# A decoder block on one core: where the mixture's last combining stands against the first group tile's work, and when two projection matrices are loaded

## What is computed

```python
# mixture (third sublayer); input is the normed x
logits = nf @ gate_weight.T + gate_bias
scores, idx = top_k(logits, 2);  w = softmax(scores)
g, lin = min(p1[..., 0::2], 7), clip(p1[..., 1::2], -7, 7)   # p1 = nf @ mlp1 + bias
act = g * sigmoid(1.702 * g) * (lin + 1)
p2 = act @ mlp2 + bias
combined = sum over the two experts of w * p2
x = x + (xc + combined)
# grouped attention (fourth sublayer), twice: groups of 32 neighbours, then of 32 strided rows
q, k, v = x @ wqs, x @ wks, x @ wvs                          # 16 heads of 64
out = softmax(q k^T / 8) v - v
x = layernorm(out @ pw + pb + x);  x = layernorm(relu(x @ w1 + b1) @ w2 + b2 + x)
```

## Time and profile before

| what | value |
|---|---|
| median of 3 runs | 2058.28 us (2058.02 to 2059.34) |
| profiled execution | 2049.87 us, span 2048.1 us |
| PE busy | 1867.4 us, 91% |
| DVE busy | 1302.1 us, 64% |
| ACT busy | 973.7 us, 48% |
| POOL busy | 966.9 us, 47% |
| DMA, mean | 59 GB/s |

### The profile page before, as it was taken

How to read it: one execution, slowest core, us unless ns; L and a number is a source line. 1 busy time by engine, 2 the same in 40 slices (tenths; PEclk the granted TensorE clock), 3 DMA queues, 4 the chain that set the end, 5 groups by cost and what they waited for, 6 DMA issues and landing times.

```text
span 2048.1 us, 52534 instructions
## 1 busy us (share of the span) xinstructions
PE 1867.4 (91%) x21476; PEld 1548.2 (76%) x21476; DVE 1302.1 (64%) x2932; ACT 973.7 (48%) x1984; POOL 966.9 (47%) x783
## 2 busy tenths in 40 slices
PE   7999999999999999977649389999999999988994
PEld 5677777777777777756437379999899999987883
DVE  6667676767676766637756565456556554556883
ACT  3666666666666666532236144334443343335551
POOL 2555555555555555535644633344234333435440
PEclk9999999999999999999869689999999999999996
DMA  7101020101230100135234520000220000220000
GB/s 245 52 17 50 19 78 19 50 19 70 101 129 19 50 11 12 40 127 167 73 101 126 153 90 13 16 20 13 80 79 28 19 18 18 71 88 17 12 17 16
DMA packets 74606, 119.85 MB, mean 59 GB/s; under 512 B 8392, under 2 KB 64464, under 8 KB 70992
## 3 DMA queue, kind: packets, MB, share of 16 engines
q1 hardware_dynamic: 69392, 105.31, 15.3%
q0 software_dynamic: 2560, 6.30, 1.1%
q10 hardware_dynamic: 2416, 4.88, 0.6%
HBM read 76.61 MB, written 39.85 MB: 57 GB/s over the span
## 4 chain that ended last, share of the span: by engine, by line
PE 41%; DVE 4%; POOL 4%; issue 3%; DMA 2%; ACT 2%; SPq 0%; POOLq 0%; DVEq 0%
PE psum L265 12%; PE psum L276 9%; PE psum L2000 4%; PE psum L1988 2%; PE psum L2492 2%; PE psum L1974 2%; PE psum L225 1%; PE psum L2526 1%; POOL b_yg L1472 1%; PE psum L1248 1%; PE psum L1338 1%; PE psum L1355 1%; POOL xs L1462 1%; PE psum L246 1%; ACT e_pr L2631 1%
## 5 line engine op out<-in xcount | busy, mean ns | idle before, releaser
L770 POOL TENSOR_TENSOR a_sm<-a_sm,a_rsum 128x1024 f32<-128x1024 f32 x256 | 480.2, 1895 | 357.1 <-DVE a_rsum L804 354.7
L792 DVE CUSTOM_DVE_ANT_0 a_sm<-psum,a_strip 128x1024 f32<-128x1024 f32 x256 | 312.1, 1219 | 145.6 <-PE psum L624 145.5
L705 ACT ACTIVATE a_sm<-a_sm,a_mn 128x1024 f32<-128x1024 f32 x256 | 293.9, 1148 | 27.3 <-DVE a_mn L792 26.2
L710 ACT ACTIVATE a_pT<-psum 128x512 f32<-128x512 f32 x256 | 151.6, 592 | 274.7 <-PE psum L637 274.7
L637 PE MATMUL psum<-ident,a_sm 128*128 128x128 f32 x2048 | 275.9, 277 | 5.7 <-POOL a_sm L770 4.6
L637 PEld LDWEIGHTS psum<-ident,a_sm 128*128 128x128 f32 x2048 | 224.4, 141 | 63.2 <-issue 46.3
L652 PE MATMUL psum<-a_pT,a_V 128*64 128x256 f32 x2048 | 249.0, 385 | 0.6 <-ACT a_o L716 0.6
L652 PEld LDWEIGHTS psum<-a_pT,a_V 128*64 128x64 f32 x2048 | 136.1, 136 | 77.3 <-issue 22.1
L799 DVE COPY a_pT<-psum 128x512 f32<-128x512 f32 x256 | 175.0, 684 | 13.3 <-PE psum L637 6.1
L2084 ACT ACTIVATE g_val<-psum 128x512 f32<-128x512 f32 x64 | 38.0, 598 | 225.5 <-PE psum L2000 225.5
L624 PE MATMUL psum<-a_KH,a_QH 64*128 64x512 f32 x512 | 114.5, 444 | 2.5 <-DVE a_mn L792 2.5
(11 more groups left out here) (394 smaller groups left out, 3733.8 us busy)
## 6 DMA issues: line engine op xcount, KB each, us to landing
a_strip<-table SPq DMA_DIRECT2D x16, 960.0 KB, 6.6
oT<-a_o SPq DMA_DIRECT2D x64, 128.0 KB, 1.9
xs<-b_zeros SPq DMA_DIRECT2D x8, 1024.0 KB, 4.1
b_oT_in<-oT SPq DMA_DIRECT2D x8, 1024.0 KB, 5.6
y<-b_yb SPq DMA_DIRECT2D x23, 256.0 KB, 2.2
b_xs<-xs SPq DMA_DIRECT2D x23, 128.0 KB, 2.2
a_raw<-in_a_wqkv SPq DMA_DIRECT2D x7, 384.0 KB, 3.3
s_x<-in_x_rev SPq DMA_DIRECT2D x4, 512.0 KB, 8.0
```

The source lines that it names most:

```text
L705: a.activation(sm[:, st % RING, :], sm[:, st % RING, :], ACT.Exp, scale=-1.0, bias=mn[:, at:at + 1], accum_out=rsum[:, at:at + 1]).then_in ...
L710: a.activation(probs(st, 0), psum[:, 4, :].rearrange("p (k q) -> p k q", k=4), ACT.Copy).then_inc(sig("pT_act"), 1)
L770: g.tensor_tensor(sm[:, st % RING, :], sm[:, st % RING, :], rsum[:, at:at + 1].broadcast_to([P, T]), ALU.mult).then_inc(sig("scaled"), 1)
L792: v.tensor_tensor_reduce(out=sm[:, st % RING, :], in0=scores_banks(hl).rearrange("p c n -> p (c n)"), in1=strip[:, pair % 2, hl, qt * P:qt ...
```

## The change

SP issues the two projection matrices in turn 5 of its unit loop (ahead of fetch_sorted(8)) and no longer ahead of the loop. At the end of the mixture, DVE does the norm sums and the scaling of tile 0 between combined(0) and combined(1), the low columns of tile 0 behind combined(1), sums, norm of tile 1 and all four key evictions of tile 0 ahead of combined(4). combined(5), (6) and (7) go into the grouped attention's step s = 0: behind the first half's `inverse`, behind the second half's `inverse`, and behind the second `transposed`. On POOL the root of tile 1 and the residual of tile 0 stand between gather(3) and gather(4), and gather(7) stands between the probabilities of the first and of the second half.

```diff
--- before.py
+++ after.py
@@ -1229,8 +1229,9 @@
         sp.wait_ge(routed("sc"), 16 * 2 * PT * NP)
         for j in range(UR):
             fetch_sorted(j)
-        then["load_projections"](sp)
         for j in range(NU + 2):
+            if j == 5:
+                then["load_projections"](sp)
             if j + UR < NU:
                 fetch_sorted(j + UR)
             if j >= 2:
@@ -1515,10 +1516,15 @@
         for r in range(UR):
             g.wait_ge(sig(f"sy{r}"), 16 * len(range(r, NU, UR)))
         g.wait_ge(sig("tables"), 2 + KC)
-        for s in range(NP):
+        for s in range(4):
             gather(s)
             if s == 1:
-                then["first_root"](g)
+                then["root"](g, 0)
+        then["root"](g, 1)
+        then["residual"](g, 0)
+        for s in range(4, 7):
+            gather(s)
+        return gather
 
     def vector(v, then):
         chain = Chain(v, sig("v_chain"))
@@ -1734,18 +1740,18 @@
         then["low_part"](v, 1)
         then["low_part"](v, 2)
         combined(0)
-        then["first_stats"](v)
+        then["first_stats"](v, 0)
+        then["first_norm"](v, 0)
         combined(1)
-        then["first_norm"](v)
+        then["low_columns"](v)
+        then["first_stats"](v, 1)
         combined(2)
-        then["low_columns"](v)
         combined(3)
+        then["first_norm"](v, 1)
+        then["first_keys"](v, (0, 1))
+        then["first_keys"](v, (2, 3))
         combined(4)
-        combined(5)
-        then["first_keys"](v, (0, 1))
-        combined(6)
-        then["first_keys"](v, (2, 3))
-        combined(7)
+        return combined
 
     return {"signals": [sig, have], "routed": routed, "where": where, "following": following, "turns": turns, "sync": sync, "tensor": tensor,
             "scalar": scalar, "gpsimd": gpsimd, "vector": vector}
@@ -2131,21 +2137,21 @@
                     high_part(a, 0, W1)
                     high_part(a, 0, W2)
 
-    def first_root(g):
-        norm_rstd(g, sig, "dl", 0, dl, mhalf)
-
-    def gpsimd(g, then):
-        def residual(s):
-            r = s % 2
-            if local(s):
-                g.wait_ge(sig("dl_h"), PT * (s + 1))
-            else:
-                loaded(g, s)
-            if s >= 2:
-                g.wait_ge(sig("dy_out"), s - 1)
-            g.wait_ge(have("vec"), 32)
-            g.tensor_tensor(eb[:, r, :, :], e[:, r, :, :], over_tiles(vec[:, phase(s), 0, :], PT), ALU.add).then_inc(sig("e_pb"), 1)
-
+    def root(g, s):
+        norm_rstd(g, sig, "dl", s, dl, mhalf)
+
+    def residual(g, s):
+        r = s % 2
+        if local(s):
+            g.wait_ge(sig("dl_h"), PT * (s + 1))
+        else:
+            loaded(g, s)
+        if s >= 2:
+            g.wait_ge(sig("dy_out"), s - 1)
+        g.wait_ge(have("vec"), 32)
+        g.tensor_tensor(eb[:, r, :, :], e[:, r, :, :], over_tiles(vec[:, phase(s), 0, :], PT), ALU.add).then_inc(sig("e_pb"), 1)
+
+    def gpsimd(g, then, gather):
         chain = Chain(g, sig("g_chain"))
 
         def result(s):
@@ -2160,7 +2166,6 @@
                 last = g.tensor_tensor(w[:, :, :], w[:, :, :], x[:, r, :, :], ALU.add)
             last.then_inc(sig("result"), 1)
 
-        residual(0)
         for s in range(NG + 1):
             front, back = s < NG, s > 0
             if back:
@@ -2172,10 +2177,12 @@
                 if s > 1:
                     g.wait_ge(sig("fy_out"), s - 1)
                 g.tensor_tensor(zb[:, :, :], z[:, :, :], over_tiles(vec[:, phase(s - 1), 3, :], PT), ALU.add).then_inc(sig("a1_b2"), 1)
-            if s + 1 < NP:
-                norm_rstd(g, sig, "dl", s + 1, dl, mhalf)
+            if 0 < s < NP - 1:
+                root(g, s + 1)
             if front:
                 for t in range(PT):
+                    if t and not s:
+                        gather(NP - 1)
                     n = PT * s + t
                     g.wait_ge(sig("d_inv"), n + 1)
                     g.tensor_tensor(pr[:, t, :, :], pr[:, t, :, :], spread(mx[:, t, :], SEG),
@@ -2184,7 +2191,7 @@
                     g.tensor_tensor(pr[:, t, :, :], pr[:, t, :, :], over_tiles(eye[:, :], H0),
                                     ALU.subtract).then_inc(sig("d_probs"), 1)
             if s + 1 < NG:
-                residual(s + 1)
+                residual(g, s + 1)
             if s == NG - 1:
                 then["first_roots"](g)
             if 0 < s < NG:
@@ -2223,7 +2230,7 @@
         v.tensor_tensor(both[:, 1, :, :], halves(banks(stage, n)), both[:, 0, :, :].bitcast(F32),
                         ALU.subtract).then_inc(sig(f"{stage}_out"), 1)
 
-    def vector(v, then):
+    def vector(v, then, combined):
         chain = Chain(v, sig("v_chain"))
 
         def shifted(s, t):
@@ -2304,12 +2311,14 @@
                 low_part(v, 1, WQ)
             if s == NP + 1:
                 low_part(v, 1, W2)
-            if s + 1 < NP:
+            if 0 < s < NP - 1:
                 first_sums(v, s + 1)
                 first_norm(v, s + 1)
             if front:
                 shifted(s, 0)
                 inverse(s, 0)
+            if not back:
+                combined(NP - 3)
             if back:
                 low_columns(v, "fT", s - 1, zT)
             if not front:
@@ -2320,6 +2329,8 @@
                 low_columns(v, "dT", s + 1, eT)
             if front:
                 inverse(s, 1)
+                if not back:
+                    combined(NP - 2)
                 transposed(s, 0)
             if back:
                 low_hidden(s - 1, (0,))
@@ -2328,6 +2339,7 @@
             if back:
                 low_hidden(s - 1, (1,))
             if not back:
+                combined(NP - 1)
                 low_part(v, 0, PW)
             if back:
                 low_hidden(s - 1, (2, 3))
...
@@ -2953,13 +2965,13 @@
 
             @block.gpsimd
             def _(g):
-                mixture["gpsimd"](g, groups)
-                groups["gpsimd"](g, last)
+                gather = mixture["gpsimd"](g, groups)
+                groups["gpsimd"](g, last, gather)
 
             @block.vector
             def _(v):
-                mixture["vector"](v, groups)
-                groups["vector"](v, last)
+                combined = mixture["vector"](v, groups)
+                groups["vector"](v, last, combined)
     return groups["signals"] + last["signals"] + [mixture["routed"]]
```

More of the change, by code:

```diff
@@ L2353, in group_attentions @@
             "high_part": lambda a, i: high_part(a, 0, i), "first_columns": lambda a: high_columns(a, 0),
-            "first_queries": lambda a, units: scaled_queries(a, 0, units), "first_root": first_root,
-            "first_stats": lambda v: first_sums(v, 0), "first_norm": lambda v: first_norm(v, 0),
+            "first_queries": lambda a, units: scaled_queries(a, 0, units), "root": root,
+            "residual": residual, "first_stats": first_sums, "first_norm": first_norm,
             "low_part": lambda v, i: low_part(v, 0, i), "low_columns": lambda v: low_columns(v, "dT", 0, eT),
```

## The result

The changed kernel took 2060.48 us (median of 22 runs, 2056.32 to 2069.71), the kernel before, run between them, 2055.3 us (22 runs, 2047.0 to 2062.66). The ratio is 1.0033, with a 95% interval of 1.0022 to 1.0045: slower by 6.8 us, between 4.5 and 9.2 (the two medians by themselves differ by 5.2, the two means by 6.4). The forecast was +0.5 us.

A forecast was written before the change was run, and what follows sets the result against it. PE, 91% busy, was taken as the bound, so only its stalls in units and seam could give time. Terms 0 - 1.7 + 1.7 + 0.5 = +0.5 us gave 2058.8 from the median 2058.28; range 2054 to 2062.5.

The forecast's parts named there:

- part one: Expert units, matrices five units later: 4.1 us gained at unit 3, lost again at unit 8; net 0, -0.9 to +1.2.
- Unit 3's fetch is then first and PE goes on: Expert units: without the matrices ahead of unit 3's fetch, PE goes on at 1056.33, saving the 3.72 us stall.
- the landing: Unit 8's fetch, behind the matrices, lands 8.4 us after the first matrix's issue, between 7.7 and 9.4.
- +1.2 at most: Expert units: the slow-side bound of the net effect of moving the matrices, forecast as 0.
- Part two: Seam, tile 0 early: projection by PW 1.7 us sooner, slower clock costs 1.7, a DVE and POOL collision 0.5.
- some 6: Front of the seam: queries start some 6 us sooner, as low columns no longer wait for gather(2).
- the end of combined(7) at 1185.1: Seam, on DVE: combined(7) follows the second half's transpose and ends 4.6 us later than before, delaying PW's load.
- The single meeting that I had priced at 0.5 us: Seam: combined(7) meets POOL's residual sum of tile 1 once, costing 0.5 us, between 0 and 1.6.
- rival (c): Seam: POOL's sums and DVE's combinings collide repeatedly, each up to 1.6 us; three give +4.3 more, 2063; chance 0.10.
- The clock: PE idle from about 1192 to 1202 drops to the 1.2 GHz level, so the projection by PW costs 1.7 us more.
- (a): Units: the matrices don't hold unit 8's fetch, the stall is gone; 4.1 us less, 2054.7; chance 0.08.
- (b): Seam: PW doesn't end it, the attention output decides; up to -10 + 1.7, about 2050; chance 0.07.

The follow-up runs named there:

- e1: Kernel before with only the two projection matrices moved to turn 5, seam unchanged; ratio 1.0007, 2057.09 us against 2053.26.
- e3: Changed kernel with PW's load issued ahead of the seventh store, its high part waiting for combined(7); ratio 1.0000, 2052.97 us.
- e6: Changed kernel with POOL's probability operations of tile 0 cut to one head of 16 and tile 1's residual sum behind combined(7); one time, 2070.55 us.
- e5: Changed kernel with PE computing queries 2 and 3 of tile 1 three times more to fill its idle gap; one time, 2070.14 us.
- f4: Same kernel as e9, run again on another chip; 2052.68 us, ratio 0.9990.
- f2: Changed kernel, unaltered, run again on another chip; 2070.41 us, one run.
- e8: Kernel before with both projection matrices issued in turn 20, behind the last fetch; ratio 0.9995, 2062.78 us against 2061.73.
- e9: Changed kernel with matrices in turn 20, PW early, first half's transpose ahead of combined(6), PW's parts behind the output's; ratio 0.9995, 2060.42 us.
- f1: Kernel before, unaltered, run again on another chip; 2057.94 us, one run.

## Why the prediction was right or wrong

The sign was right and 2060.5 lies inside the range. But +0.5 us was forecast, less than can be told from no change, and +6.8 was measured, which is more. That the number falls in the range is luck: the forecast stood on the median of three runs of the kernel before, 2058.28, and over 22 runs that median is 2055.3. As a difference the range went from -4.3 to +4.2 us, and +6.8 is outside it. By the stages, units and seam together are +8.1 us in the first pair of traces. The means are +2.6 for the units (80.4 with the matrices ahead in three traces, 83.0 with them in turn 5 in six) and +5.9 for the seam (78.7 in five traces of the old order, 84.6 in three of the changed one, those with the creeping left out).

**Step by step, part one.** "Unit 3's fetch is then first and PE goes on" was right. So was the mechanism at unit 8, which waits for the fetch behind the matrices. The term that failed is the landing: I took 8.4 us with ends of 7.7 and 9.4; it was 9.9 in the profiled run, 10.5 in e1, and never under 9.5 in the six traces. The row of unit 3 that I had as the far end was the better one. So PE stood 5.5 to 6.3 us where I had 3.8. The profiled run's 4.22 looks close only because another 1.34 us were waited at unit 7, whose fetch, issued ahead of the matrices, was held too; I had excluded that by looking at the queue's order only. And the slow round behind the stall took 4.57 us, not 3.85. "+1.2 at most" was thus too narrow: unit 8's transposes stood on average 25.1 us behind unit 0's in the three traces with the matrices ahead and 26.9 in the six with them in turn 5, and the stage as a whole is 2.6 longer.

**Part two, the front.** Queries 6.3 us sooner, where "some 6" stood. Scores at 1169.76, which is 34.4 us behind the first gather; 1165 would have been 34.2. POOL through its gathers 40.9 us behind the first one, as summed to 1171.8. All right.

**Part two, the path to PW.** Here the sum broke. It had the end of combined(7) at 1185.1, 54.3 us behind the first gather; it came at 1194.00, 58.7 behind. The 4.4 us are made of these:
- the softmax of the first half was ready 0.7 us later than POOL, which the text allowed for: +0.7;
- gather(7) waited 1.41 us for combined(5), whose buffer it needs: +1.4. combined(5) had been stretched by 1.7 us by POOL's own two operations, and without that its buffer would have been free before POOL was. I had put gather(7) directly behind them;
- both transposes stood behind combined(6), 3.2 us stretched by three operations of POOL. In my sum a single transpose of 0.8 us followed POOL's last probability operation at once. Here the pair began 1.9 us after that operation's end at 1188.23 and took 1.3: +2.4.

The single meeting that I had priced at 0.5 us, combined(7) with the residual sum, did not occur: by then the residual sum had met combined(6). So this is rival (c), with its place (POOL's operations amid the combinings), its price (1.7 and 3.2 us for the two groups) and its result, everything behind gather(7) and combined(7) late by as much. I gave it 0.10 because the gather issues had kept their length beside the same combinings. They did so again (0.95 us); but what counts is the arithmetic operations, and the change puts five of them, four on the probabilities and the residual sum of tile 1, exactly where DVE combines. The forecast's mechanism, PW late behind combined(7), is right as well: both hold, one on top of the other, and e3 and e6 show each by itself.

The Trainium skill (SBUF — State Buffer, section SBUF: two separate sides) states the exclusive lock as a rule, among others for a DVE operation with two inputs in SBUF against a GpSimd operation that reads SBUF. By it every one of these meetings counts, and the runs side with it: combined(6) lost 3.2 us beside 3.83 us of POOL's work (1.06 + 1.33 + 1.44), and nothing in e6 beside narrow operations. The prediction weighed the rule, and then counted one meeting, because it gave combined(5) and combined(6) no place in time. It also read the 2.31 us of the earlier trace rows as agreeing with the rule since the loss of 1.6 us exceeds POOL's 1.27. The rule doesn't say that, and it gives the pair to whichever starts first, while that row of DVE starts at 1174.40, ahead of POOL's 1174.88; the measurement stands, and how the two share is not settled by it.

**From the store to the projection.** Store to load 4.9 us, where 5.3 stood. PW's load took 6.3 us instead of 4.8: +1.5. From its landing to the projection 6.7 us; the sum had 6.8. In total the projection stood 3.8 us later instead of 1.7 sooner, and the missing 5.5 are, to rounding, the 4.4, the 1.5 and the -0.4. Why the load takes longer is open. It took 6.0 to 6.8 us in all eight traces with the changed order at the seam and 4.7 to 4.9 in all six with the old one. The later time is not the reason: e3 issues it 55.3 us behind the first gather, as the kernel before does at 55.0, and it still took 6.4.

**The clock.** Right in kind, near in size: PE idle for 9.82 us where "about 10" stood, a granted clock of 0.50, the 1.2 GHz level, at the projection's start, and 8.06 us for it. Against the 5.92 before, that is 2.1 us where 1.7 was put, and e5 shows it to be the idle time.

**The rivals on the fast side.** (a) fell: unit 8 stalled in every trace with turn 5. (b), that PW doesn't end the seam, fell too, and e3 adds that with PW's load out of the way only 0.9 us of gain was to be had in this order of DVE's work. With the first transpose ahead of combined(6) and PW's parts behind the output's as well, f4 gained 5 us of the seam.

## What to carry to other kernels

Before moving DVE's work among POOL's, lay both timelines over each other and charge every pair of arithmetic operations that will overlap with most of the length of the other (here 1.7 of 2.3 us and 3.2 of 3.8); a gather issue in the same slot cost next to nothing here. Follow a moved operation through its buffers as well as its queue: gather(7) waited for combined(5) by its double buffer, not by its place. A bulk load moved along a queue of small, just-in-time fetches only moved its stall here, until it went behind the last of them. And where whole runs scatter more than the effect, cut the traces in stages that start and end at the edit.

## What was not expected of the hardware

**A small fetch can be held by megabytes issued behind it.** 128 KB issued 1.3 us ahead of two 1 MB loads on the same queue landed after 3.9 us in the changed kernel's trace, and e5 shows the same. In e1, e3 and f2 the same fetch, issued as far ahead, landed after 2.0 to 2.2 us. The visible difference is SP's issue of the first load, which lasted 1.56 us in the changed kernel and 1.75 in e5 and 0.47 in the others; the cause stays open. Issued behind the loads, the fetch landed 9.6 to 10.5 us after the first load's issue in all six traces. Pieces of 256 KB between the fetches still cost 1.9 us at one unit.

**PE can creep without a visible cause.** On one chip, in all four traces from it (e5, e6, e8, e9), and in none of the ten others, PE started one to four matmuls at a time for 8 to 15 us while POOL issued its gathers. PE's timeline of e8, which there has the same code as the kernel before:

```profile
1167.83 0.28 PE L265 MATMUL psum<-g_eT,g_wq 128*128 128x256 f32 x1 [1.14 <-issue]
...
1174.13 0.37 PE L265 MATMUL psum<-g_eT,g_wk 128*128 128x256 f32 x1 [2.42 <-issue]
...
1181.16 7.46 PE L265 MATMUL psum<-g_eT,g_wk 128*128 128x256 f32 x41 [0.36 <-issue]
```

The waits are for issue and nothing that the profile names. The kernel before had a median of 2061.73 us there and of 2053.26 and 2054.93 on two others. f1 to f4, without it on another chip, speak for the chip rather than for the order of the work; the cause stays open.
